# A four-layer graph network: join weights, reciprocals and intermediate rows between attention layers moved from SBUF to PSUM

## The reference

```python
def gat_conv(x, ei, W, a_src, a_dst, b, heads, out_ch):
    h = (x @ W).reshape(n, heads, out_ch)
    alpha_src = jnp.sum(h * a_src, axis=-1)
    alpha_dst = jnp.sum(h * a_dst, axis=-1)
    e = leaky_relu(alpha_src[src] + alpha_dst[dst], 0.2)
    m = segment_max(e, dst); ex = exp(e - m[dst]); s = segment_sum(ex, dst)
    out = segment_sum(ex / (s[dst] + 1e-16) * h[src], dst)
    return out.reshape(n, heads * out_ch) + b
h = elu(gat_conv(x, ei, W1, as1, ad1, b1, 8, 16))   # a self loop is added for each node
h = elu(gat_conv(h, ei, W2, as2, ad2, b2, 8, 16))
h = gat_conv(h, ei, W3, as3, ad3, b3, 1, 64)
h = h @ Wp + bp                                      # and divided by its norm
```

## Time and profile before

| | us |
|---|---|
| median of 3 runs | 21263.13 |
| lowest, highest | 21261.28, 21264.03 |
| the profiled execution | 21308.26 |
| its span | 21306.4 |

### The profile page before, as it was taken

How to read it: one execution, slowest core, us unless ns; L and a number is a source line. 1 busy time by engine, 2 the same in 40 slices (tenths; PEclk the granted TensorE clock), 3 DMA queues, 4 the chain that set the end, 5 groups by cost and what they waited for, 6 DMA issues and landing times. The chain is left out here.

```text
span 21306.4 us, 279817 instructions
## 1 busy us (share of the span) xinstructions
PE 11122.1 (52%) x78780; PEld 9729.5 (46%) x78780; DVE 7699.8 (36%) x27111; ACT 5288.4 (25%) x13270; POOL 10896.9 (51%) x11299
## 2 busy tenths in 40 slices
PE   5555533555555595344443344542455554777775
PEld 4444422333333595344442344442344443666664
DVE  5444443444444454333335233334222223222222
ACT  2444422343343331111111111111111111222221
POOL 3666655444444203555555555556555553555552
PEclk8665656666666796566665566665555555888886
DMA  3333321111111252222222222222111111222221
GB/s 126 122 119 123 118 70 57 53 53 51 53 53 52 89 184 82 72 94 91 94 91 76 76 92 93 91 94 64 41 45 46 46 45 42 86 89 87 90 90 41
DMA packets 825864, 1693.45 MB, mean 79 GB/s; under 512 B 374630, under 2 KB 453813, under 8 KB 784369
## 3 DMA queue, kind: packets, MB, share of 16 engines
q0 software_dynamic: 361120, 580.47, 10.6%
q1 hardware_dynamic: 356481, 526.01, 7.8%
q10 hardware_dynamic: 107776, 582.40, 7.0%
HBM read 853.52 MB, written 863.86 MB: 81 GB/s over the span
## 5 line engine op out<-in xcount | busy, mean ns | idle before, releaser
L112 POOL DMA_INDIRECT eg_got<-gat_table,eg_rows x4992 | 4738.4, 949 | 3333.9 <-issue 1459.1
L112 POOL DMA_INDIRECT e_got<-table,e_rows x3328 | 3150.6, 947 | 2202.5 <-issue 919.8
L1381 PE MATMUL eg_ps_sum<-eg_got,eg_equal 128*128 128x136 f32 (+1 forms) x9984 | 2283.8, 402 | 2154.4 <-DVE eg_got L1505 1753.6
L1381 PEld LDWEIGHTS eg_ps_sum<-eg_got,eg_equal 128*128 128x128 f32 x9984 | 2091.8, 303 | 2263.5 <-issue 2217.4
L117 POOL DMA_INDIRECT sorted_rows<-sort_rows,sort_dest x1664 | 1612.6, 969 | 2159.9 <-ACT sort_rows L975 1121.6
L1358 DVE TENSOR_TENSOR eg_equal<-eg_ps_key,eg_key 128x512 f32<-128x512 f32 x1248 | 863.1, 692 | 4359.6 <-remote 2041.6
L1388 ACT ACTIVATE eg_outs<-eg_ps_sum 128x544 f32<-128x544 f32 (+1 forms) x1248 | 666.1, 543 | 4048.7 <-PE eg_ps_sum L1381 1947.3
L1368 PE MATMUL eg_ps_key<-ident,eg_key 128*128 128x128 f32 x4992 | 1189.0, 386 | 186.9 <-DVE eg_key L1350 186.5
L941 PE MATMUL sort_ps_table<-sort_hot 128*128 128x128 bf16 x1664 | 422.9, 254 | 1619.1 <-issue 669.1
L963 ACT ACTIVATE sort_dist<-sort_ps_hi,iota_part 128x128 f32<-128x128 f32 x1664 | 611.5, 367 | 2028.6 <-remote 1291.6
L1438 PE MATMUL eg_small<-eg_cut,eg_equal_b 128*128 128x8 bf16 (+1 forms) x14976 | 599.7, 168 | 918.6 <-issue 907.5
(11 more groups left out here) (514 smaller groups left out, 25836.4 us busy)
## 6 DMA issues: line engine op xcount, KB each, us to landing
gat_out<-eg_outs ACTq DMA_DIRECT2D x208, 1152.0 KB
out<-e_outs ACTq DMA_DIRECT2D x208, 512.0 KB
out<-e_outs ACTq DMA_DIRECT2D x104, 1024.0 KB
values_q<-e_zeros_b SPq DMA_DIRECT2D x104, 768.0 KB
sort_value<-values_q SPq DMA_DIRECT2D x104, 768.0 KB
eg_got<-gat_table,eg_rows POOLq DMA_INDIRECT x4992
gat_out<-eg_outs ACTq DMA_DIRECT2D x104, 528.0 KB
e_rows<-sorted_rows SPq DMA_DIRECT2D x104, 520.0 KB
```

The costliest lines, as they stand in the source:

```text
L112: return e.indirect_dma_start(out, None, table, bass.IndirectOffsetOnAxis(ap=index, axis=0), **kw)
L1381: last_i = e.matmul(ps_sum[q % 2][:, i, 0:FG], equal[k % NE][:, t, :], got[k][:, t, :], start=True, stop=True)
```

## The change

`Merge` gets a flag `in_psum`. `gat_next` sets it: `ea`, `eb` and the intermediate rows `f` are then views of one PSUM tile `mg_ps` of four banks (1,792 + 2 x 112 numbers a partition), with which the stage fills all eight banks. `GatClose` loses its tile `inv` and uses `ea` for the reciprocal in its place, in all three closes, and writes the scaled rows to `f` in place of `feat` before the bias is added. In `GatOpen`, thus also in `b1c`, both products read the PSUM result directly, and the copy moves behind the first reduction.

```diff
@@ gat_next
-        close = GatClose(self, ph, n, heads, ch, *tables, out, ring=1)
+        close = GatClose(self, ph, n, heads, ch, *tables, out, ring=1, in_psum=True)
@@ class Merge, __init__
-        self.top, self.ea, self.eb, self.sb = (ph.sb(f"mg_{k}", [P, n, heads]) for k in ("m", "a", "b", "s"))
-        self.f = ph.sb("mg_f", [P, n, heads * ch])
+        self.top, self.sb = (ph.sb(f"mg_{k}", [P, n, heads])[:, :, :] for k in ("m", "s"))
+        if in_psum:
+            HF, w = n * heads * ch, n * heads
+            banks = ph.ps("mg_ps", [P, -(-(HF + 2 * w) // BANK) * BANK])
+            self.f = banks[:, 0:HF].rearrange("p (t c) -> p t c", t=n)
+            self.ea, self.eb = (banks[:, HF + i * w:HF + (i + 1) * w].rearrange("p (t h) -> p t h", t=n) for i in B2)
+        else:
+            self.ea, self.eb = (ph.sb(f"mg_{k}", [P, n, heads])[:, :, :] for k in ("a", "b"))
+            self.f = ph.sb("mg_f", [P, n, heads * ch])[:, :, :]
@@ GatClose.vector
-        own_h, a, e_own, inv = self.hid[j % self.ring], self.agg[:, ts, :], self.e_own[:, :, :], self.inv[:, :, :]
+        own_h, a, e_own, inv = self.hid[j % self.ring], self.agg[:, ts, :], self.e_own[:, :, :], self.merge.ea
...
         e.reciprocal(inv, inv).then_inc(ve, 1)
         e.wait_ge(ve, c(1))
-        e.tensor_tensor(by_head(f, heads), by_head(a[:, :, 0:HF], heads), over(inv, ch), ALU.mult).then_inc(ve, 1)
+        e.tensor_tensor(by_head(self.merge.f, heads), by_head(a[:, :, 0:HF], heads), over(inv, ch), ALU.mult).then_inc(ve, 1)
         e.wait_ge(ve, c(1))
-        e.tensor_tensor(f, f, across(self.bias[:, :], CHUNK), ALU.add).then_inc(ve, 1)
+        e.tensor_tensor(f, self.merge.f, across(self.bias[:, :], CHUNK), ALU.add).then_inc(ve, 1)
@@ GatOpen, project
+            e.tensor_tensor(s_prod, ps[:, :, :], across(self.a_src[:, :], k), ALU.mult).then_inc(out, 1)
+            e.tensor_tensor(d_prod, ps[:, :, :], across(self.a_dst[:, :], k), ALU.mult).then_inc(out, 1)
+            e.wait_ge(out, 5 * b + 1)
+            e.reduce_sum(hid[:, :, HF:FG], by_head(s_prod, heads), axis=AX.X).then_inc(out, 1)
             e.tensor_copy(hh, ps[:, :, :]).then_inc(out, 1)
-            e.wait_ge(out, 5 * b + 1)
-            e.tensor_tensor(s_prod, hh, across(self.a_src[:, :], k), ALU.mult).then_inc(out, 1)
             e.wait_ge(out, 5 * b + 2)
-            e.reduce_sum(hid[:, :, HF:FG], by_head(s_prod, heads), axis=AX.X).then_inc(out, 1)
-            e.tensor_tensor(d_prod, hh, across(self.a_dst[:, :], k), ALU.mult).then_inc(out, 1)
-            e.wait_ge(out, 5 * b + 4)
             e.reduce_sum(self.dst[:, ts, 0:heads], by_head(d_prod, heads), axis=AX.X).then_inc(out, 1)
```

More of the change, by code:

```diff
@@ L2133, in vector @@
                     close.vector(e, j)
-                    elu.vector(e, self.feat[:, CHUNKS[j], 0:HF], close.merge.f[:, :, :])
+                    elu.vector(e, self.feat[:, CHUNKS[j], 0:HF], close.merge.f)
                     e.sem_inc(closed, 1)
@@ L2145, in scalar @@
                 if j < n_chunks:
-                    elu.scalar(e, close.merge.f[:, :, :])
+                    elu.scalar(e, close.merge.f)
         ph.run(sync=sync, gpsimd=gpsimd, tensor=tensor, vector=vector, scalar=scalar)
@@ L2567, with __init__ @@
 class Merge:
[L2570 removed]
+    def __init__(self, ph, n, heads, ch, in_psum=False):
         self.heads, self.ch = heads, ch
[L2572 to L2573 removed]
+        self.top, self.sb = (ph.sb(f"mg_{k}", [P, n, heads])[:, :, :] for k in ("m", "s"))
[7 more added lines that the diff above has]
+            self.f = ph.sb("mg_f", [P, n, heads * ch])[:, :, :]
         self.ve, self.below, self.exped = (ph.sem(f"mg_{k}") for k in ("ve", "below", "exped"))
@@ L2580, in vector @@
         to_acc, to_s, to_m = to[:, :, 0:HF], to[:, :, HF:HF + heads], to[:, :, HF + heads:HF + 2 * heads]
-        top, ea, eb, sb, f = self.top[:, :, :], self.ea[:, :, :], self.eb[:, :, :], self.sb[:, :, :], self.f[:, :, :]
+        top, ea, eb, sb, f = self.top, self.ea, self.eb, self.sb, self.f
         n = self.calls(1)
@@ L2605, in scalar, with __init__ @@
         e.wait_ge(self.below, 2 * n)
-        e.activation(self.ea[:, :, :], self.ea[:, :, :], ACT.Exp).then_inc(self.exped, 1)
-        e.activation(self.eb[:, :, :], self.eb[:, :, :], ACT.Exp).then_inc(self.exped, 1)
+        e.activation(self.ea, self.ea, ACT.Exp).then_inc(self.exped, 1)
+        e.activation(self.eb, self.eb, ACT.Exp).then_inc(self.exped, 1)
 class GatClose:
-    def __init__(self, kn, ph, n, heads, ch, table, own, out, ring=2):
+    def __init__(self, kn, ph, n, heads, ch, table, own, out, ring=2, in_psum=False):
         self.kn, self.heads, self.ch, self.HF, self.table, self.own, self.ring = kn, heads, ch, heads * ch, table, own, ring
@@ L2619, in __init__ @@
         self.dst = ph.sb("own_dst", [P, NT, HEADS])
-        self.e_own, self.inv = ph.sb("e_own", [P, CHUNK, heads]), ph.sb("inv", [P, CHUNK, heads])
+        self.e_own = ph.sb("e_own", [P, CHUNK, heads])
         self.bias = ph.sb("bias", [P, HF])
-        self.merge = Merge(ph, CHUNK, heads, ch)
+        self.merge = Merge(ph, CHUNK, heads, ch, in_psum)
         self.collect = Collect(kn, ph, self.agg, 0, out, m_from=FG)
```

## The result

The changed kernel took 21,386.28 us (median), the kernel before on the same chip 21,264.03 us. The ratio is 1.0056 [1.0044, 1.0067]: slower by 0.56%, or 122 us between the medians, where no change that can be measured was forecast. Some executions are 4 to 5% slower at a lower granted clock; the ratios leave these out. Repeated in a second comparison at that level it was 1.0058 [1.0041, 1.0075]. The profiled execution has a span of 21,388.7 us, 82 us over that of before, whose profiled execution lay 45 us above its median.

The account below looks back on a forecast made before the run. DVE's chain up to opening chunk 5 (g1c, g2c) or 6 (b1c) was taken to set the stage ends. g1c -0.2, g2c +1.6 and b1c -9.4 gave -8.0 us, so 21,255 us, range 21,228 to 21,284.

Parts of the forecast that it names:

- The operations: Close and ELU in g1c, g2c: L2554 and L2556 take 2.02 us each, other costs small; +13.9 us a stage.
- The rival of a kept two-element rate: g1c, g2c: writing PSUM keeps the two-element rate, only L2554 can; 13 us less, 21,242; chance 0.12.
- that of half-rate writes: g1c, g2c: DVE writes PSUM at half rate, four operations a chunk, 105 us more, 21,360; chance 0.04.
- The projection: GatOpen in b1c, g1c, g2c: batch starts 0.60 us apart; -9.4, -9.0 and -7.2 us.
- That the stretch goes with one operand in PSUM: g1c, g2c: POOL's indirect DMAs fall to about 0.98 to 1.00 us; worth 5.1 us a stage.
- The rival in which POOL stays stretched: g1c, g2c: POOL stays stretched despite one PSUM operand; each stage 3.1 us worse, 21,261; chance 0.12.
- The wait before chunk 1: g1c: DVE's 5.09 us wait for gathers before chunk 1 goes; -5.1 us, the same taken for g2c.
- own_rows: g1c, g2c: DVE's idle 8.7 us for this load in each of five chunks stays, within 1 us a chunk.
- Where POOL's relief ends: Collecting stages: other POOL relief becomes longer waits for DVE, in g1c above 18.62 us before the sixth chunk's scatters; no gain.
- the sum: Changed stages: g1c 13.9 - 9.0 - 5.1 = -0.2, g2c +1.6, b1c -9.4; total -8.0 us.
- The rival that POOL is the true bound: g1c, g2c: all POOL's relief comes through, 48 us in g1c, twice that with g2c, 21,159; chance 0.03.

Follow-up runs that it names:

- the projection alone: The kernel before with only the change's GatOpen part (both products read PSUM, copy moved back), merge left in SBUF: 0.9989 on the upper level, 0.9988 on the lower.
- pauses put back: The changed kernel with a 128x2400 memset on POOL after each 14 closing gathers in g1c and g2c: 0.9998 [0.9989, 1.0008] on the upper level.
- the repeat: The kernel before, unchanged, run and profiled again on the upper level: 0.9997 [0.9988, 1.0007].

## Why the prediction was wrong, point by point

- **The operations: right.** L2554 and L2556 2.03 us for 2.02; PSUM writes of two-input operations nothing; ScalarE 47 ns cheaper, where I took no change. The rival of a kept two-element rate and that of half-rate writes are both out.
- **The projection: right.** The starts in a batch, in g1c:

```profile
11498.76 0.69 DVE L2799 TENSOR_TENSOR g1c_open_tmp<-g1c_open_ps_o,g1c_a_src 128x512 f32<-128x512 f32 x1 [0.25 <-issue]
11499.36 0.68 DVE L2800 TENSOR_TENSOR g1c_open_tmp<-g1c_open_ps_o,g1c_a_dst 128x512 f32<-128x512 f32 x1
11499.96 0.68 DVE L2802 TENSOR_REDUCE g1c_agg<-g1c_open_tmp 128x32 f32<-128x512 f32 x1
```

  0.60 us apart where the earlier trace rows had 0.73; b1c was 11.2 us shorter for 9.4 forecast; alone it gave 0.9989 and 0.9988 at the two levels, for a forecast of 0.9988 (-25.6 us).
- **That the stretch goes with one operand in PSUM: right**, and more fully than the nearest row told: mean gather 1280 to 997 ns. The rival in which POOL stays stretched is out. The Trainium skill ("SBUF — State Buffer", section "Who interferes with whom") has it that a VectorE instruction with at most one SBUF input, outside the two-port modes, does not contend with GpSimd. This trace agrees: 997 ns.
- **The wait before chunk 1: right.** It is gone; in the projection alone, on the lower level, it stands at 5.0 us.
- **own_rows: right**, 8.7 to 9.2 us a chunk in g1c, and in g2c 55.9 us in five for 59.5 before, less than 1 us a chunk.
- **Where POOL's relief ends: right as far as it goes.** Its waits for DVE before scatters in g1c grew from 22.5 to 131.5 us, the one before the sixth chunk's from 18.62 to 24.55.
- **The step that failed** is the sentence "All other relief of POOL falls before a wait for DVE and turns into a longer one". It puts all of POOL's relief but the 5.1 us wait at nothing. I let the relief end as idle time of POOL and asked only when POOL's transfers would be done, never what POOL's denser issue does to the other engines. It made the gathers of g1c an unbroken row from 11391.9 to 11519.1, and in and just behind it the results of TensorE reached ScalarE and DVE up to 52 us late. The term that I took as zero measured 60.3 us of new waits in g1c and made g2c 59.5 us longer, for 122 between the medians. With pauses put back the same kernel stands at 0.9998. Its g1c and g2c take 327.5 and 322.4 us, 10.5 and 9.2 over those of the projection alone on the same chip, where the sum had 8.8 in each; so the sum's other terms hold within 2 us. (Against the first trace of before it is +1.3 and +8.4, for -0.2 and +1.6 in the sum; but g2c of the kernel before had itself 314.0 us in one profile and 319.3 in the other.) No rival had this; the one that ended slower had the wrong mechanism, a PSUM write at half rate, at 0.04.
- **It stood in the profile.** In b1c, 8200 to 8420 us, where POOL gathers with little of DVE beside it, the waits of the kernel before are:

```profile
DVE feat L2063 <- remote: 97.9, 7, 32.7
ACT b1c_lin_src_t L2461 <- DMA b0c_bias<-in_L_gnn_b: 67.5, 5, 27.4
```

  A releaser that is not on this core in a program on one core, and the load of a bias of an earlier stage: neither is one, and both instructions wait for TensorE. I had read b1c from its end only.
- **The rival that POOL is the true bound** has its answer too: POOL was relieved by 48 us in g1c and none of it came through, even with pauses.

The version that beats both kernels at both levels is the projection alone, by a tenth of a per cent (0.9989 and 0.9988, with intervals that end at 0.9998 and 0.9999). With pauses of POOL in all collecting stages it is 0.9919 on the upper level, but pauses gain nothing on the lower.

## What to carry to other kernels

Before an engine is made faster, ask what its slowness leaves room for. A row of indirect DMAs that is stretched by a neighbour costs its own time, but the stretch may be what lets the others' signals through; a relief that is worthless by the chain of waits isn't thereby harmless. In a trace, an idle stretch whose named releaser was long done, or is "remote", beside an engine that issues without a hole, is a term to be priced for each stage in which the change would make such a row. And where chips differ by a quarter of the time, no ratio holds until it is measured on both kinds.

## What the runs showed of the hardware

- On chips where the kernel before takes some 21,300 us, TensorE's recorded work reaches its waiting readers 11 to 52 us late in and just behind a long row in which POOL issues indirect DMAs 1.30 us apart (0.98 to 1.00 us each, 0.30 between). In the row shown the results of its first 44 us were not late, and one was late still 6 us after its end. One memset of 2.12 us after each 14 leaves waits of at most 8.7 us, and the time they had cost is gone. With gathers stretched to about 1.6 us from start to start by DVE's operations the longest such wait in g1c was 1.7 us, in the repeat 4.6. On chips where the same kernel takes some 16,300 us no such wait was seen in g1c, in a row as unbroken (mean gather 1004 ns). Whether TensorE ends its work late or only its signals are late can't be told, since the ends of its matmuls are modelled; and what makes the chips differ is open.
- DVE with an output in PSUM: 128x1792 of two inputs in 2.02 us, as into SBUF; a tensor_scalar 2.03 us, from SBUF to PSUM as well as from and to PSUM, for 1.09 in SBUF.
- POOL's indirect DMAs beside DVE operations that have an operand in PSUM take 0.98 to 1.00 us each; beside the same operations with all operands in SBUF their means were 1.19 us (scatters) and 1.28 (gathers).
